# Layer normalisation in a four-layer graph network: one over the root as Exp of minus half the Ln on ScalarE, in place of Sqrt on ScalarE and a reciprocal on VectorE

## What is computed

```python
def _layernorm(x, axis=-1, eps=1e-05):
    m = jnp.mean(x, axis=axis, keepdims=True)
    v = jnp.var(x, axis=axis, keepdims=True)
    return (x - m) / jnp.sqrt(v + eps)

x = x + _L0_gnn_ref(_layernorm(x), edge_index, ...)        # attention
x = x + _L0_ffn_ref(_layernorm(x)[None], ...)[0]           # experts
x = x + _L1_gnn_ref(_layernorm(x), edge_index, ...)        # message passing
x = x + _L1_ffn_ref(_layernorm(x)[None], ...)[0]           # splines
```

## Time and profile before

| | us |
|---|---|
| median of 3 runs | 2235.35 (2234.48 to 2235.82) |
| the profiled execution | 2243.05 |
| its span, first to last instruction | 2241.3 |
| busy in the span: PE / PEld / DVE / ACT / POOL | 1940.6 / 1481.8 / 1346.8 / 1100.6 / 645.2 |
| mean granted TensorE clock, as a share of full speed | 0.951 |
| the reciprocals of the three calls, 9 instructions | 24.8 |

### The profile page before, as it was taken

The page is one execution under the profiler, slowest core; times in us unless marked ns, Lnnn a source line. Parts: engine busy times, 40 slices in busy tenths (PEclk is TensorE's granted clock), DMA queues, the critical chain, the costliest instruction groups (busy, mean ns, idle before and its releaser), DMA issues. The chain is left out here.

```text
span 2241.3 us, 35000 instructions
## 1 busy us (share of the span) xinstructions
PE 1940.6 (87%) x10201; PEld 1481.8 (66%) x10201; DVE 1346.8 (60%) x1861; ACT 1100.6 (49%) x1719; POOL 645.2 (29%) x468
## 2 busy tenths in 40 slices
PE   4875997979889999999967769999899984899998
PEld 2554443445467777777755358888668854798997
DVE  6783788154257667777601535555433349999996
ACT  2663664221157667667600146666322226767664
POOL 3001100007644334444275067777200005000000
PEclk8998998979989999999989889999999997999999
DMA  2202931113168769787555167777301140000001
GB/s 85 80 14 53 364 91 51 35 55 103 13 228 306 272 224 331 283 304 281 180 151 175 40 159 188 193 194 186 86 28 34 38 167 2 1 1 1 1 1 47
DMA packets 121605, 282.66 MB, mean 126 GB/s; under 512 B 51616, under 2 KB 58778, under 8 KB 111966
## 3 DMA queue, kind: packets, MB, share of 16 engines
q1 hardware_dynamic: 53646, 189.25, 24.7%
q0 software_dynamic: 67792, 91.34, 14.4%
HBM read 242.05 MB, written 53.89 MB: 132 GB/s over the span
## 5 line engine op out<-in xcount | busy, mean ns | idle before, releaser
L2070 PE MATMUL ps<-ft,kw 128*128 128x157 f32 x2304 | 327.6, 301 | 38.6 <-DVE ft L1994 24.4
L2070 PEld LDWEIGHTS ps<-ft,kw 128*128 128x128 f32 x2304 | 314.3, 191 | 52.7 <-DVE ft L1994 31.5
L1157 POOL DMA_INDIRECT xg<-nrows,idx x128 | 211.4, 1651 | 271.4 <-PE ps L1183 242.0
L1475 POOL DMA_INDIRECT pg<-prows,srcI x170 | 209.9, 1234 | 79.0 <-issue 46.2
L1506 PE MATMUL ps<-ehot,msg 125*128 125x125 f32 x1360 | 164.4, 280 | 17.2 <-ACT ehot L1598 11.4
L1506 PEld LDWEIGHTS ps<-ehot,msg 125*128 125x128 f32 x1360 | 158.9, 195 | 30.4 <-issue 19.2
L1196 PE MATMUL ps<-wh,xh 128*128 128x512 f32 x364 | 151.6, 416 | 6.3 <-DVE xl L1314 4.5
L2018 ACT ACTIVATE ksq<-ksrc,kn 128x942 f32<-128x942 f32 (+2 forms) x120 | 110.1, 920 | 94.5 <-DVE cube L1977 94.3
L1301 DVE TENSOR_TENSOR wgl<-wexp,wh 128x2048 fp32r<-128x2048 f32 x64 | 146.6, 2290 | 0.3 <-issue 0.3
L1241 ACT ACTIVATE wh<-wexp 128x2048 fp32r<-128x2048 f32 x64 | 122.6, 1917 | 44.3 <-PEq L838 44.3
L1196 PE MATMUL ps<-wgl,xh 128*128 128x512 f32 x364 | 143.2, 393 | 0.0
(11 more groups left out here) (298 smaller groups left out, 4265.5 us busy)
## 6 DMA issues: line engine op xcount, KB each, us to landing
wexp<-wexp_d SPq DMA_DIRECT2D x64, 1024.0 KB
wexp<-wexp_d SPq DMA_DIRECT2D x64, 512.0 KB
yrows<-y SPq DMA_DIRECT2D x91, 256.0 KB
yrows<-nought POOLq DMA_DIRECT2D x1, 16384.0 KB, 57.2
attr<-attr_d SPq DMA_DIRECT2D x42, 250.0 KB
kw<-kw_d SPq DMA_DIRECT2D x2, 4608.0 KB
qs<-qk SPq DMA_DIRECT2D x32, 156.2 KB, 6.8
ks<-qk SPq DMA_DIRECT2D x32, 156.2 KB, 7.2
```

The source lines that it names most:

```text
L1157: pool.indirect_dma_start(xg[:, e % 2, h, :], None, d["nrows"], bass.IndirectOffsetOnAxis(ap=idx[:, 2 * e + h:2 * e + h + 1], axis=0), bou ...
L1475: pool.indirect_dma_start(pg[:, p % 4, t % 2, :], None, d["prows"], bass.IndirectOffsetOnAxis(ap=c.srcI[:, t:t + 1], axis=0)).then_inc(s_g ...
L2070: mm = pe.matmul(c.ps[:, bank + m // 2, m % 2 * CB:m % 2 * CB + CB], w[:, k, f, m * P:m * P + P], ft[:, f % RF, a:a + CB], start=False, st ...
```

## The change

In `layernorm`, ACT writes the logarithm of `var + eps` into `rstd`, waits for it (a new semaphore `s_log` in place of `s_std`), and takes the exponential of -0.5 times it in place, which is one over the root. DVE's three reciprocals go, and with them its wait for its own reciprocal: its multiplications now wait for ACT's exponential. The fourth normalisation, inside attention, keeps its root and reciprocal (L481, L536), and so does the small root of `cell_inputs`.

```diff
-        s_mean, s_cent, s_sq, s_var, s_std, s_rstd = (
-            c.sem(name + n) for n in ("mean", "cent", "sq", "var", "std", "rstd"))
+        s_mean, s_cent, s_sq, s_var, s_log, s_rstd = (
+            c.sem(name + n) for n in ("mean", "cent", "sq", "var", "log", "rstd"))
...
                 for i, (a, w) in enumerate(SPANS):
-                    dve.wait_ge(s_std, i + 1)
-                    dve.reciprocal(rstd[:, a:a + w], rstd[:, a:a + w]).then_inc(s_rstd, 1)
                     dve.wait_ge(s_rstd, i + 1)
                     dve.tensor_tensor(c.nT[:, :, a:a + w], c.nT[:, :, a:a + w], all_k(rstd[:, a:a + w], w), ALU.mult)
...
                 for i, (a, w) in enumerate(SPANS):
                     act.wait_ge(s_var, i + 1)
-                    act.activation(rstd[:, a:a + w], var[:, a:a + w], ACT.Sqrt, bias=c.eps[:, 0:1])\
-                        .then_inc(s_std, 1)
+                    act.activation(rstd[:, a:a + w], var[:, a:a + w], ACT.Ln, bias=c.eps[:, 0:1]).then_inc(s_log, 1)
+                    act.wait_ge(s_log, i + 1)
+                    act.activation(rstd[:, a:a + w], rstd[:, a:a + w], ACT.Exp, scale=-0.5).then_inc(s_rstd, 1)
```

## The result

| | before | changed |
|---|---|---|
| median of 5 runs, us | 2234.54 (2234.27 to 2235.82) | 2226.74 (2219.88 to 2229.82) |
| ratio to before, 95% interval | | 0.9954, 0.9939 to 0.9970 |
| the profiled execution, us | 2243.05 | 2226.90 |
| its span, us | 2241.3 | 2225.2 |
| busy, us: DVE / ACT | 1346.8 / 1100.6 | 1320.4 / 1124.5 |

The forecast was 2225.15 us, in a range of 2220 to 2230.5. Three of the five runs of the kernel before are those of the table ahead of the prediction. The ratio corresponds to 10.3 us, its interval to 6.7 to 13.6 us; the difference of the two medians is 7.8 us. The changed kernel's runs scatter over 10 us where the five of the kernel before lay within 1.6 us; on the chips of the experiments both scatter by 10 to 16 us.

A forecast was written before the change was run, and what follows sets the result against it. Each normalisation block was bound by DVE's reciprocals and multiplications, moving to ACT; 15.90 - 12.50 = 3.40 us a call, 10.2 us for three, takes the median from 2235.35 to 2225.15 us, range 2220 to 2230.5.

The forecast's parts named there:

- The tail: Each layernorm call from first table load to DVE's last multiplication: 15.90 us would become 12.50, a gain of 3.40.
- All five durations: Durations assumed in the calls: load 1.28 us, Ln 0.69 and 0.45, Exp 0.63 and 0.39.
- The loads outside: Routing's own load goes without gain; the small root in cell_inputs gets one, covered by 13 us, at no cost.
- A: Table switches in the calls cost more than recorded: 2244.4 us in full (0.06), 2229.6 in small form (0.12 shared with C).
- B: One load would serve both Ln and Exp: 7.7 us gained a call, 2212 us; chance 0.01.
- C: Late weights of the third call or a later stage take gain back: 2228.6 us; chance 0.12 shared with small A.
- D: PE keeps 2.4 GHz into the stages behind the first two calls: 4.8 us more gain, 2220.3 us; chance 0.06.
- The step from the profiled execution to the median: Timed runs were taken as 7.70 us below the profiled execution: 2232.85 us profiled, 2225.15 median.
- the last of its own signs: The forecast is wrong if the stages behind the calls do not keep their length.
- The chances: Probabilities given to the outcomes: forecast range 2223 to 2227 got 0.73, faster (below 2230.9) got 0.88.

The follow-up runs named there:

- e5: The kernel before with Ln and Exp in the third call alone, the first two calls keeping root and reciprocal: 2220.89 us, ratio 0.9985.
- e9: The changed kernel reordered to four table loads a call, the first hidden by an early one-column Ln, on the third experiment chip: 2227.33 us, ratio 0.9906.
- e8: The changed kernel without an edit, run again on the third experiment chip: 2240.01 us, ratio 0.9957 to the kernel before.
- e4: The kernel before without an edit, run again on the second experiment chip: 2221.65 us, ratio 0.9991 to the other runs of itself.

## Why the prediction was right

**The tail.** All five durations held: load 1.283, Ln 0.69 and 0.45, Exp 0.63 and 0.39 us. The trace gave 12.47 us for a sum of 12.50, the other calls 12.48, and so 3.43 us a call for 3.40. The prices came from ACTIVATEs of other functions with the same size and kind of operands, and the earlier trace rows.

**The loads outside.** Routing's Exp lost its load and gained nothing: it waits for DVE all the same, as its row in the trace after shows.

```profile
481.13 0.74 ACT L947 ACTIVATE rex<-rex 125x640 f32<-125x640 f32 x1 [3.53 <-DVE rex L975]
```

In `cell_inputs` the new load and the root end 12.2 us before DVE asks for the result; these answer to the earlier trace rows:

```profile
1593.80 1.28 ACT L1641 ACT_TABLE_LOAD   x1 [4.08 <-PEq L1457]
1595.10 0.30 ACT L1641 ACTIVATE sc<-par,eps 128x4 f32<-128x4 f32 x1
...
1607.57 0.17 DVE L1664 RECIPROCAL sc<-sc 128x4 f32<-128x4 f32 x1
```

**The rivals.** A, the dearer switch, is out in both forms. The gaps at the 18 loads of the calls are 0.02 us, and with six, four, two and one loads the tails came out within 0.05 us of a chain that charges each load its 1.28 us and nothing else. By the trace, then, the drain of 1.38 us that the Trainium skill ("ScalarE: Activation LUTs", section "What ACT_TABLE_LOAD costs") states for each switch is not there in this kernel. B was worked out right, at 8.2 us, but only for a kernel without the switches; the build did not use a table common to Ln and Exp. C, a gain taken back, is out for the third call by e5 and by the splines, which take 383.7 to 383.9 us in every kernel. Behind the first two calls the stages vary by more than the gain of a call, so there only the totals speak, and a microsecond or two given back would not show in them. D is out in the place it named: routing's first matmuls start at 1.2 GHz, as the windows behind the first call show (length, PE, PEld, DVE, ACT, POOL, clock, DMA share, GB/s), which answer to the earlier trace rows:

```profile
460.00:465.00 5.00, 0.00 (x0) 0.00 (x0) 2.32 (x2) 4.87 (x6) 0.00 (x0) 0.57 0.00 0
...
466.00:470.00 4.00, 3.62 (x5) 1.16 (x6) 0.68 (x2) 0.00 (x0) 2.09 (x8) 0.50 0.10 34
470.00:472.00 2.00, 2.00 (x5) 0.56 (x4) 0.00 (x0) 0.00 (x0) 0.00 (x0) 0.77 0.00 0
```

The matmuls start at 466.38, and the mean of 0.77 in 470 to 472 puts the rise at 470.9, so that the low stretch is 4.5 us long, for the 4.8 that I read before. Behind the second call it is 3.6 us after the change and 4.2 before. At half rate these differences are worth 0.5 us together at most, and D had asked for 4.8.

**What was wrong.** The step from the profiled execution to the median. I treated the 7.70 us between them as a constant of the kernel and predicted 2232.85 us for the profiled execution; it took 2226.90. Single executions differ by as much in every group of runs (e9's profiled execution is 8.84 us above its median). Between traces these differences lie in attention, the heads, the expert stage and the edge network; in which of them the 7.70 us lay is not known, because the timed runs leave no trace. The forecast for the median did not suffer, because only a difference entered it. I also took the surroundings of a call for fixed, and did not put in the range that each head alone can move by 1.7 us.

By the last of its own signs the forecast would even have been wrong, since the stages behind the calls did not keep their length: the edge network is 4.0 us shorter in the first trace. The repeated runs show that this is variation between executions, so the sign was badly chosen and the mechanism stands. The chances were not added up right either: the cases that end below 2230.9 make 0.92, not 0.88.

**What was luck.** The mechanism and its size are shown by the tails. That the median came within 1.6 us of the forecast is partly luck, since the runs of the changed kernel scatter over 10 us and the interval of the ratio allows any gain from 6.7 to 13.6 us.

## What to carry to other kernels

Where two functions come from different tables, do not count the loads but follow the chain to the last consumer: a load in an engine's idle time is free (attention, `cell_inputs`, the early Ln), one on the way costs its 1.28 us, and grouping calls by table can lose if it makes the first result wait for the last input. Before such a change, look at the built order for where the compiler puts the loads. When a gain is half a per cent and executions scatter by as much, cut the trace into stages that repeat exactly and stages that do not, and judge the change by the first kind. Before counting all the work that a change removes, look which part of it the next consumer waits for: in attention it was one reciprocal of three.

## What the runs showed of the hardware

The heads of the first two calls fall into two lengths, 12.2 and 13.7 to 13.9 us, with the same instructions. The granted clock shows why. Around the start of the first call before the change it is still at 2.4 GHz, then falls to 1.2 GHz while the mean's matmuls run, and comes back 4 us into the call (the first row is the stretch ahead of it):

```profile
437.80:441.80 4.00, 2.10 (x12) 1.74 (x11) 1.10 (x1) 0.90 (x2) 0.00 (x0) 1.00 0.00 0
441.80:442.80 1.00, 0.97 (x3) 0.49 (x4) 0.00 (x0) 0.00 (x0) 0.00 (x0) 0.96 0.13 7
442.80:445.80 3.00, 3.00 (x5) 1.34 (x4) 0.00 (x0) 0.00 (x0) 0.00 (x0) 0.50 1.05 298
```

After the change the same matmuls, behind the same 1.92 us of idle PE, ran at 2.4 GHz throughout:

```profile
441.30:445.60 4.30, 4.23 (x10) 2.00 (x11) 0.52 (x1) 0.00 (x0) 0.00 (x0) 1.00 0.76 232
```

In the second call it was the other way round, with a mean of 1.00 before and 0.67 after:

```profile
1225.70:1230.00 4.30, 4.21 (x10) 2.00 (x11) 0.51 (x1) 0.00 (x0) 0.00 (x0) 1.00 0.72 259
```

```profile
1219.00:1223.30 4.30, 4.29 (x7) 1.99 (x8) 0.00 (x0) 0.00 (x0) 0.00 (x0) 0.67 0.73 253
```

The fall comes in some executions of a kernel and not in others (e8 and the changed kernel in the first call), so it is no effect of the change. The third call, behind 7.68 us of idle PE, is at 1.2 GHz already when its matmuls start, in every trace. Its head takes 14.9 to 15.3 us, but for one of 13.7 us (e4), where the clock came back about 3 us into the call and not over 5.

```profile
1826.40:1830.70 4.30, 4.20 (x5) 1.85 (x6) 0.00 (x0) 0.00 (x0) 0.00 (x0) 0.50 0.83 274
```

The edge network, which gathers rows for 21250 edges, takes 350 to 352, 361 to 365, 336 to 341 and 361 to 366 us in the four groups of the table: it goes with the group and not with the kernel. The last three groups ran on three chips, and the first group's chip is not known, so that the chip and the time of the run are not told apart. Between the groups the wait of POOL for DVE ahead of its gathers differs (19 us in e4, 46 us in e8), while DVE's own wait for the gathered rows is 8.5 and 8.4 us. What sets it was not found out.
